# Sum over heads: from four GpSimd additions per slot into SBUF to one adding DMA per slot into device memory

## The reference, cut to what matters

```
q, k, v, w = silu(causal conv of width 4 over x @ W)     16 heads x 128
per head: a gated scan over the 512 tokens gives o_t (128 values per token and head)
o = rms_norm(o) * norm_w * sigmoid(gate)
attention = sum over the heads of (o_head @ Wo_head)      512 x 256 per sequence
x1 = layernorm(x + attention)
out = layernorm(x1 + ffn(x1))
```

## Time and profile before

| | |
|---|---|
| median of 3 runs | 2137.21 us (2136.2 to 2137.25) |
| the profiled execution's own time | 2138.05 us |
| its span, first to last instruction | 2136.1 us |
| busy: PE, DVE, POOL, ACT | 1961.0, 1750.6, 1430.1, 1401.1 us |
| mean granted TensorE clock | 0.975 |
| all of GpSimd's additions to `acc` (L556) | 178.8 us, 256 of them, 731 ns each |
| bytes moved by DMA | 20.68 MB, a mean of 10 GB/s |

### The profile page before, as it was taken

How to read it: one execution, slowest core, us unless ns; L and a number is a source line. 1 busy time by engine, 2 the same in 40 slices (tenths; PEclk the granted TensorE clock), 3 DMA queues, 4 the chain that set the end, 5 groups by cost and what they waited for, 6 DMA issues and landing times.

```text
span 2136.1 us, 41666 instructions
## 1 busy us (share of the span) xinstructions
PE 1961.0 (92%) x12064; PEld 1609.5 (75%) x12064; DVE 1750.6 (82%) x4091; ACT 1401.1 (66%) x3935; POOL 1430.1 (67%) x2461
## 2 busy tenths in 40 slices
PE   7799999999999999999999999999999999997676
PEld 6578777777778787777777787877777777775565
DVE  1788888888888888888888888888888888883555
ACT  2566777767767767777677777677776776773332
POOL 4367676777777776767777777767677777765233
PEclk8899999999999999999999999999999999998798
DMA  2000000000000000000000000000000000000000
GB/s 62 11 2 1 16 2 14 3 15 3 15 3 15 3 2 16 2 15 2 15 3 15 2 15 3 1 16 1 15 3 15 3 15 3 5 1 7 11 20 20
DMA packets 41737, 20.68 MB, mean 10 GB/s; under 512 B 13745, under 2 KB 41521, under 8 KB 41521
## 3 DMA queue, kind: packets, MB, share of 16 engines
q1 hardware_dynamic: 41520, 18.10, 3.1%
HBM read 15.99 MB, written 2.10 MB: 8 GB/s over the span
## 4 chain that ended last, share of the span: by engine, by line
PE 70%; DVE 12%; issue 8%; POOL 7%; ACT 2%; DMA 1%; DVEq 0%; SPq 0%; POOLq 0%; ACTq 0%
PE proj_ps L609 15%; PE mix_ps L693 11%; PE V_ps L664 8%; PE work_ps L721 7%; PE work_ps L727 6%; PE tr_ps L633 4%; DVE conv L479 4%; PE V_ps L642 3%; PE proj_ps L1281 3%; PE mix_ps L700 2%; PE work_ps L713 2%; DVE A L602 2%; PE proj_ps L1312 2%; POOL fused_lo L879 2%; DVE U L461 2%
## 5 line engine op out<-in xcount | busy, mean ns | idle before, releaser
L479 DVE SCALAR_TENSOR_TENSOR conv<-proj_ps,coefs,conv 128x511 f32<-128x511 f32 (+2 forms) x768 | 563.4, 734 | 11.3 <-ACT conv L334 4.3
L300 POOL TENSOR_TENSOR W<-W,tot 128x256 f32<-128x256 f32 x384 | 273.1, 711 | 200.1 <-PE mix_ps L693 200.1
L693 PE MATMUL mix_ps<-W,U 128*128 128x128 f32 x1792 | 299.9, 289 | 54.0 <-DVE A L602 41.4
L828 POOL TENSOR_TENSOR A_lev<-A,masks 128x256 f32<-128x256 f32 x448 | 322.9, 721 | 10.7 <-ACT A L377 10.7
L693 PEld LDWEIGHTS mix_ps<-W,U 128*128 128x128 f32 x1792 | 256.0, 191 | 91.4 <-DVE A L597 52.8
L664 PE MATMUL V_ps<-A_lev,UT 128*128 128x128 f32 x1792 | 284.2, 281 | 26.0 <-DVE V_ps L574 25.9
L602 DVE COPY_PREDICATED A<-masks,mix_ps 128x256 f32<-128x256 uint32 x448 | 268.2, 599 | 8.7 <-PE mix_ps L693 8.7
L664 PEld LDWEIGHTS V_ps<-A_lev,UT 128*128 128x128 f32 x1792 | 235.6, 191 | 51.5 <-DVE V_ps L574 51.3
L472 DVE TENSOR_TENSOR wT<-wT,tot 128x128 f32<-128x128 f32 x768 | 223.1, 331 | 41.9 <-DVE U L461 1.4
L574 DVE TENSOR_TENSOR V_ps<-V_ps,tot 128x256 f32<-128x256 f32 x384 | 164.9, 429 | 91.5 <-PE V_ps L664 91.2
L609 PE MATMUL proj_ps<-hT_hi,w_hi 128*128 128x512 f32 x512 | 223.1, 436 | 8.7 <-DVE conv L479 7.4
(11 more groups left out here) (175 smaller groups left out, 4738.5 us busy)
## 6 DMA issues: line engine op xcount, KB each, us to landing
acc<-in_L_attn_hidden_states SPq DMA_DIRECT2D x1, 2048.0 KB, 8.6
w_raw<-in_L_attn_Ww SPq DMA_DIRECT2D x16, 128.0 KB, 2.3
w_raw<-in_L_attn_Wq SPq DMA_DIRECT2D x16, 128.0 KB, 2.4
w_raw<-in_L_attn_Wk SPq DMA_DIRECT2D x16, 128.0 KB, 2.4
w_raw<-in_L_attn_Wv SPq DMA_DIRECT2D x16, 128.0 KB, 2.4
wo_raw<-in_L_attn_Wo SPq DMA_DIRECT2D x16, 128.0 KB, 2.2
out_x<-acc SPq DMA_DIRECT2D x4, 512.0 KB, 2.9
wf_head<-in_L_attn_Wf SPq DMA_DIRECT2D x16, 64.0 KB, 1.9
```

Of the source, the lines that this page charges most:

```text
L300: nc.gpsimd.tensor_tensor(w, w, block_tot(u3.par, lev, 0), ALU.mult).then_inc(W_step, 1)
L479: nc.vector.scalar_tensor_tensor(y_, proj_ps[:, CONV_BANK[i], 0:T - back], filt(u, i, KW - 1 - back), y_, ALU.mult, ALU.add).then_inc(conv ...
L693: last = nc.tensor.matmul(mix_ps[:, half, p * P:(p + 1) * P], Ulev(u3, lev)[:, p * P:(p + 1) * P], after_odd(W[:, p * T // 2:(p + 1) * T / ...
L828: nc.gpsimd.tensor_tensor(dst, diag_after_odd(lev), mask_cols(lev), ALU.mult)\
```

## The change

The running sum moves from SBUF to a new tensor `head_sum` in device memory (128 rows x 16 KB). SP fills it once with x, by a copy from device memory to device memory. In place of GpSimd's four additions, GpSimd waits for all four tiles of `y_sb` and for the adding DMA of the unit before, and issues one DMA that adds `y_sb` (512 KB) to its quarter of `head_sum`. ScalarE's wait at L545 is now for that DMA. After the last one SP loads the 2 MB back into `acc`, ahead of the feed-forward loads, and VectorE's layer norm waits for this load. The transposes at the start still read x from `acc`.

```diff
         def scale_output(act, u4, t):
             if t == 0:
                 act.wait_ge(rms_step, u4.count(4, 4))
-                wait(act, acc_done, u4.count(4, 0))
+                wait(act, acc_done, u4.count(16, 0))
...
-        def add_heads_output(pool, u5, t):
-
-            pool.wait_ge(ys_done, u5.count(4, t + 1))
-            wait(pool, acc_done, u5.count(4, -12 + t))
-            a = acc[:, u5.par * C + t, :]
-            nc.gpsimd.tensor_tensor(a, a, y_sb[:, t, :], ALU.add).then_inc(acc_done, 1)
+        def add_heads_output(pool, u5):
+
+            pool.wait_ge(sum_set, 16)
+            pool.wait_ge(ys_done, u5.count(4, 4))
+            wait(pool, acc_done, u5.count(16, 0))
+            nc.gpsimd.dma_start(head_sum[:, u5.par * C:(u5.par + 1) * C, :], y_sb[:, :, :], accum_op=ALU.add)\
+                .then_inc(acc_done, 16)
...
+        head_sum = nc.dram_tensor("head_sum", [P, NT * HID], F32, kind="Internal").ap().rearrange("p (t n) -> p t n", n=HID)
...
             nc.sync.dma_start(wb_raw, Wb.rearrange("(k p) n -> p k n", p=P)).then_inc(w_in, 16)
+            nc.sync.dma_start(head_sum[:, :, :], x.rearrange("b (c p) n -> p (b c) n", p=P)).then_inc(sum_set, 16)
             for i, c in enumerate((cv, cq, ck)):
...
-            sp.wait_ge(acc_done, 4 * B * H)
+            sp.wait_ge(acc_done, 16 * B * H)
+            nc.sync.dma_start(acc[:, :, :], head_sum[:, :, :]).then_inc(sum_in, 16)
...
                     if s.u5 and i == 0:
-                        for t in range(C):
-                            add_heads_output(pool, s.u5, t)
+                        add_heads_output(pool, s.u5)
...
-            dve.wait_ge(acc_done, 4 * B * H)
+            dve.wait_ge(sum_in, 16)
```

More of the change, by code:

```diff
@@ L193, in build @@
         names = ("x_in w_in small_in flip_ready head_w head_f head_g head_q head_k head_v head_o const_ready mask_ready xT_ps xT_hi xT_lo "
-                 "setup_hi setup_lo first_ps first_sb beta_step norm_set wo_scaled high_done low_done gbias_set "
+                 "setup_hi setup_lo first_ps first_sb beta_step norm_set sum_set sum_in wo_scaled high_done low_done gbias_set "
                  "proj_ps_ready gate_ps_ready wT_ps_ready vT_ps_ready A_ps_ready UT_ps_ready V_ps_ready KV_ps_ready s_ps_ready "
@@ L201, in build @@
         (x_in, w_in, small_in, flip_ready, head_w, head_f, head_g, head_q, head_k, head_v, head_o, const_ready, mask_ready, xT_ps,
-         xT_hi, xT_lo, setup_hi, setup_lo, first_ps, first_sb, beta_step, norm_set, wo_scaled, high_done, low_done,
+         xT_hi, xT_lo, setup_hi, setup_lo, first_ps, first_sb, beta_step, norm_set, sum_set, sum_in, wo_scaled, high_done, low_done,
          gbias_set,
```

## The result

The changed kernel takes 2147.73 us (median of 5 runs, 2146.43 to 2149.35); the kernel before, in the same comparison, 2137.25 us. The ratio is 1.0047, with a 95% interval of 1.0033 to 1.0062. The forecast was 2147 us and slower. In the profiled executions the span went from 2136.1 to 2147.3 us, +11.2 us.

A forecast was written before the change was run, and what follows sets the result against it. TensorE was 70% of the chain of waits, GpSimd 7%, counting only where something waits for it. Terms 0 + 0 + 0.1 + 3.7 + 5.8 + 0 = +9.6 us on 2137.2 gave 2147 us; range 2140 to 2180 us.

The forecast's parts named there:

- Part 1: Middle slots: removing GpSimd's additions gains 0.6 us over 61 slots, rounded to 0; bounds 0 and 29 us.
- Part 2: 64 DMA issues on GpSimd, about 1 us each, cost 0; at 4.20 us each they would cost 50 us.
- T: Time GpSimd is held by one DMA issue, taken as 1 us.
- The threshold of 3.38 us: How long an issue may hold GpSimd at no cost: 2.79 us of freed additions plus 0.59 us of slack.
- Part 3: ScalarE's scaling waits for the adding DMA, hidden except in slot 66: +0.1 us, bounds 0 to +3.2 us.
- L: Adding DMA's time from issue to landing, taken as 5.5 us: 2.9 plain, 1.9 for reading the destination, the rest software.
- The window of 16.3 us: Time from the adding DMA's place of issue to ScalarE's next scaling, within which its landing is hidden.
- rival (b): Adding DMA lands later than 16.3 us, so ScalarE's scaling is late in each slot; about 2400 us; 6%.
- Part 4: Behind the last scaling, SP waits for the last adding DMA to land: +3.7 us, bounds +1.1 to +6.8.
- Part 5: The 2 MB load back ahead of the six loads delays VectorE's start by 5.8 us; bounds +1.7 to +8.6.
- Part 6: Copy of x into head_sum at the start, hidden ahead of head 0's weights: 0, bounds 0 and +8.6 us.
- rival (a): The issue holds GpSimd over 3.38 us, delaying the second grow_W in 61 slots; 2197 us at 4.20 us; 12%.

The follow-up runs named there:

- e1: The kernel before with GpSimd's 256 additions left out and nothing in their place; 2133.9 us, ratio 0.9982.
- e2: The changed kernel with two of the four old additions kept behind the DMA issue on GpSimd; 2150.18 us, ratio 1.0057.
- e3: The changed kernel with all four old additions kept behind the DMA issue on GpSimd; 2176.28 us, ratio 1.0178.
- e8: The changed kernel with GpSimd's DMA storing y_sb plainly in place of adding it; 2143.52 us, timed once.
- e4: The changed kernel without the load of the sum back into acc (the norm works on x); 2141.45 us, ratio 1.0016.
- e5: The changed kernel with the load back moved behind the six small loads in SP's list; 2149.74 us, ratio 1.0051.

## Why the prediction was right

The mechanism was right: the middle slots did not change, and the landing of the last adding DMA and the load back are what the change costs. That the time came within 1 us is in part luck, as misses of opposite sign cancelled.

- **Part 1, the middle slots: right.** 62 slots differ by 0.05 us in all, and in e1, without any additions, by 0.46 us.
- **Part 1, what was left out.** I took slots 3 and 7 for all slots. Slot 65 has no u2: there TensorE has little else to do, so GpSimd is on the path. The changed kernel gained 1.58 us there and 0.34 in slot 64. TensorE's wait for the second `grow_W` shows 1.00 us of it, 2.03 us before and 1.03 us after.

```profile
1952.18 1.19 PE L693 MATMUL mix_ps<-W,U 128*128 128x128 f32 x4 [2.03 <-POOL W L300]
```

```profile
1951.45 1.20 PE L694 MATMUL mix_ps<-W,U 128*128 128x128 f32 x4 [1.03 <-POOL W L300]
```

The other 0.6 us came at the end of the stretch, where TensorE does the same work at another clock. Its last four products for `mix_ps` took 1.06 us before and 0.61 after, and the windows from 1960 to 1962 us, before and then after, show a granted clock of 0.50 (the lower level, 1.2 GHz) and 0.85. In e1 the clock had risen by then too (0.98 from 1958 to 1960 us). Why it rises earlier is not shown.

```profile
1960.00:1962.00 2.00, 2.00 (x7) 1.64 (x7) 0.48 (x1) 0.04 (x1) 0.63 (x1) 0.50 0.03 8
```

```profile
1960.00:1962.00 2.00, 2.00 (x11) 1.60 (x9) 0.48 (x2) 0.84 (x2) 0.67 (x2) 0.85 0.03 8
```

- **Part 2, the issue: right.** T = 0.92 us against 1 us. The threshold of 3.38 us lies where e2 and e3 leave room for it. e3's price per slot (0.37 us for 3.74 us, an excess of 0.36) looks like one for one, but most of it is the slower second `grow_W`, so the price above the threshold is not measured cleanly.
- **Part 3, mis-sized.** L was 6.4 us, not 5.5: the term for reading the destination was 1.9 us and measured 3.4 us (e8); the term for software, 0.7 us, measured 0.1. The sum also let the DMA be issued as soon as the unit was scaled; the issue came 1963.64 - 1963.13 = 0.51 us later. So ScalarE waited in slot 66: +1.44 us where the sum had 0.1, inside its bound of 3.2. The window of 16.3 us was never near, so rival (b) falls.
- **Part 4, mis-sized by the same term.** +5.23 us for +3.7. Beside L, GpSimd's issue came 1972.24 - 1971.71 = 0.53 us after the last scaling, which the sum had left out here as well.
- **Part 5: right.** +5.84 us for +5.8, 12.91 us for 12.7. e4 takes 5.4 of them away, and e5 shows that another order gains nothing. What held the small loads back stands in SP's rows: the last of the six is issued 1987.97 - 1978.71 = 9.26 us after SP goes on, against 1976.89 - 1973.35 = 3.54 before. That is 5.72 of the 5.84 us, and the issues of `sg_sb` and `su_sb` (3.61 and 3.17 us in place of 0.58 and 1.43) are 4.77 of it.
- **Part 6: right.** The copy took 11.8 us, between the 8.6 and 17.2 us given for it, and nothing waits for it: it delays the last weight issue of head 0 from 17.11 to 23.70 us, long before the 50 us at which they are wanted, and x landed as before. Its part in the clock after 55 us is open.
- **The sum.** 9.6 us forecast; +11.2 us in the profiled executions, of which 0.66 is the start, and +10.5 us between the medians. The gain left out (1.9 us) cancels two thirds of what parts 3 and 4 had too small (1.3 + 1.5 us). The forecast's own range should have begun at 2140 us: the lower bounds of parts 3 to 5 are 0 + 1.1 + 1.7 us, while 2141.5 us is only where a difference can be told.
- **The rule on the fixed cost.** e8's plain store from GpSimd landed in 3.0 us. The Trainium skill's fit ("DMA: Bandwidth & Descriptors", Anatomy of one DMA) gives an estimate of 3.2 us for it, and the trace agrees; for the adding DMA it is off by a factor of two, and the measurement decides.
- **The added point of rival (a).** That GpSimd's descriptors are held up while VectorE runs a copy in a two-port mode (the Trainium skill, "SBUF — State Buffer", the box on the trap in which VectorE blocks such a DMA) no run here shows. The predicated copies named in the prediction start some 4 us after the issue. The one issue that overlaps such a copy, at 1948.81 us in slot 65, took 0.94 us; all 64 took 0.91 to 1.05 us.

## What to carry to other kernels

Look in the trace of before for a stretch in which the work in question is already missing, such as the first slot of a pipeline: it measures the gain without a run. But look also at the slots that drain the pipeline, where less stands beside the same work. An engine's freed time is worth what waits for it. Work that leaves an engine as DMA was paid here where nothing hides a DMA, in the last two units and in the load back.

## What the runs showed of the hardware that was not expected

- An adding DMA of 512 KB from SBUF to device memory lands in 6.4 us, a plain one of the same shape in 3.0 us. Its packets take 10.7% of the 16 engines' span in place of 3.8%, with the same count and bytes.
- The issue itself is longer with the addition: a median of 0.92 us of GpSimd in place of 0.64 us, for the same 128 rows of 4 KB.
- The bytes read on the page of the profile do not hold the destination: it gives 20.19 MB read from device memory after and 15.99 before. The difference, 4.2 MB, is the copy and the load back; 33.56 MB were added to. e8, which adds nothing, has the same 20.19 MB.
